# Edge MLP of a graph network: attribute product over 128 rows, bias added on the way out of PSUM, sums three groups behind, padding rows spread

## The reference

```
for i in range(4):
    ef  = silu(concat(h[row], h[col], edge_attr) @ edge_w1[i] + edge_b1[i])
    ef  = silu(ef @ edge_w2[i] + edge_b2[i]) * edge_mask
    agg = segment_sum(ef, row, n)
    h   = (h + silu(concat(h, agg) @ node_w1[i] + node_b1[i]) @ node_w2[i] + node_b2[i]) * node_mask
```

## Time and profile before

| | |
|---|---|
| median of three runs | 8339.4 us (8332.0 to 8347.34) |
| span of the profiled execution | 8339.0 us |
| TensorE matmul busy | 6397.8 us (77%) |
| VectorE busy | 4889.1 us (59%) |
| ScalarE busy | 2862.7 us (34%) |
| GpSimd busy | 5197.0 us (62%) |
| first `eat` product (L1650) of L1 to the last | 2294.4 to 5827.6 us |

### The profile page before, as it was taken

The page is one execution under the profiler, slowest core; times in us unless marked ns, Lnnn a source line. Parts: engine busy times, 40 slices in busy tenths (PEclk is TensorE's granted clock), DMA queues, the critical chain, the costliest instruction groups (busy, mean ns, idle before and its releaser), DMA issues. The chain is left out here.

```text
span 8339.0 us, 233485 instructions
## 1 busy us (share of the span) xinstructions
PE 6397.8 (77%) x55084; PEld 5290.0 (63%) x55143; DVE 4889.1 (59%) x13551; ACT 2862.7 (34%) x8539; POOL 5197.0 (62%) x7407
## 2 busy tenths in 40 slices
PE   2222215767699998999899989999976666888998
PEld 1111113555477776888688868887475556887998
DVE  6333346867556654666466646665432225998998
ACT  3222202545333333333333333333233332222554
POOL 3777755756477776777577757776577774222554
PEclk7555556555599999999999999999555556999999
DMA  5000013434388886888688868887300001332232
GB/s 163 3 3 3 3 38 113 120 96 121 94 223 216 216 204 179 222 222 222 164 222 222 222 163 226 222 222 184 100 6 7 7 7 35 82 82 56 72 73 59
DMA packets 1322718, 1020.15 MB, mean 122 GB/s; under 512 B 479756, under 2 KB 1223586, under 8 KB 1321696
## 3 DMA queue, kind: packets, MB, share of 16 engines
q1 hardware_dynamic: 938010, 667.14, 29.1%
q0 software_dynamic: 134272, 178.98, 11.0%
q10 hardware_dynamic: 250308, 172.51, 7.1%
HBM read 951.88 MB, written 73.77 MB: 123 GB/s over the span
## 5 line engine op out<-in xcount | busy, mean ns | idle before, releaser
L1607 POOL DMA_INDIRECT qg<-q_tab,qidx x2520 | 2388.6, 948 | 928.8 <-issue 692.8
L1762 DVE COPY ps<-b 128x384 f32<-128x384 f32 x1120 | 628.1, 561 | 1355.7 <-ACT h L1727 1348.1
L1156 PE MATMUL ps<-rhs_i,ohi 128*128 128x128 f32 (+2 forms) x8640 | 1215.5, 266 | 210.3 <-issue 198.3
L1156 PEld LDWEIGHTS ps<-rhs_i,ohi 128*128 128x128 f32 (+1 forms) x8640 | 999.1, 162 | 343.2 <-issue 281.9
L1122 POOL COPY near<-x 128x48 bf16 x2160 | 676.0, 351 | 775.9 <-PE ps L1145 433.2
L1676 PE MATMUL ps<-ohm,h 128*128 128x128 f32 x6720 | 1032.1, 290 | 61.3 <-DVE ps L1762 30.7
L1307 POOL DMA_INDIRECT got_m<-y_tab,idx_m x832 | 832.9, 1001 | 344.6 <-issue 246.3
L1720 ACT ACTIVATE h<-ps,b 128x384 f32<-128x384 f32 x1120 | 651.2, 581 | 1049.3 <-PE ps L1658 964.1
L1676 PEld LDWEIGHTS ps<-ohm,h 128*128 128x128 f32 x6720 | 838.5, 191 | 252.0 <-issue 237.0
L406 POOL DMA_INDIRECT list_by_src<-ring,rpos x808 | 783.0, 969 | 333.0 <-issue 254.2
L1781 DVE TENSOR_SCALAR ohm<-iota_row,loc_p,w_p 128x128 f32<-128x128 f32 x3360 | 963.1, 354 | 0.1
(11 more groups left out here) (441 smaller groups left out, 8601.8 us busy)
## 6 DMA issues: line engine op xcount, KB each, us to landing
pb<-p_tab ACTq DMA_DIRECT2D x1680, 96.0 KB
pb<-p_tab SPq DMA_DIRECT2D x1680, 96.0 KB
places<-place_by_turn SPq DMA_DIRECT2D x560, 192.0 KB
places_i<-place_by_meeting SPq DMA_DIRECT2D x360, 256.0 KB, 3.4
places_i<-place_by_meeting SPq DMA_DIRECT2D x720, 128.0 KB, 3.1
qb<-q_tab SPq DMA_DIRECT2D x840, 64.0 KB
qg<-q_tab,qidx POOLq DMA_INDIRECT x2520
nears<-near_by_turn SPq DMA_DIRECT2D x560, 64.0 KB
```

Of the source, the lines that this page charges most:

```text
L1156: m = pe.matmul(ps[:, bass.ds(to[j], width)], ohi[:, h, j, :], rhs[:, h, j, 0:width], start=False, stop=True, skip_group_check=True)
L1607: pool.indirect_dma_start(qg[:, h, j, :], None, q_tab, IndirectOffsetOnAxis(ap=qidx[:, h, j:j + 1], axis=0)).then_inc(m_got[h], 16)
```

## The change

Four things. The `eat` and `we36` tiles become 128 rows high, with rows 36 to 127 zeroed once before the layers, and the product L1650 reads all 128 rows. The bias b2 is no longer seeded into PSUM: VectorE's `add(n)` reads z2, adds b2 and writes h2 in SBUF, and then writes zeros to z2 behind a wait for its own add; ScalarE's silu goes from h2 to h2. `sums` runs three groups behind instead of two, `build_m` two behind instead of one. The padding records get the local node p (their partition), and where the column is beyond the table it becomes p instead of 3199.

```
--- before.py
+++ after.py
-                        dve.memset(padt[:, :, 1:2], FAR).then_inc(s_pad, 1)
+                        v_chain(dve, dve.memset(padt[:, :, 1:2], FAR))
+                        dve.tensor_scalar(padt[:, :, 0:1], padt[:, :, 0:1], iota_p[:, 0:1], None, ALU.add).then_inc(s_pad, 1)
...
                         dve.tensor_copy(loc_p[:, at], banks[4][:, 0:HN])
-                        dve.tensor_scalar(col_p[:, at], banks[5][:, 0:HN], float(NP - 1), None, ALU.min)
+                        then(dve.tensor_copy(col_f[:, 0, :], banks[5][:, 0:HN]))
+                        then(dve.scalar_tensor_tensor(col_f[:, 1, :], col_f[:, 0, :], float(NP), col_f[:, 0, :], ALU.is_lt, ALU.mult))
+                        then(dve.tensor_scalar(col_f[:, 0, :], col_f[:, 0, :], float(NP), iota_p[:, 0:1], ALU.is_ge, ALU.mult))
+                        dve.tensor_tensor(col_p[:, at], col_f[:, 0, :], col_f[:, 1, :], ALU.add)
...
-                eat = sb(f"eat{layer}", [36, U3, GW], BF16, st)
...
                         def second(k, h):
                             n = k * U3 + h
-                            pe.wait_ge(m_seed, s0 + 2 + n)
+                            if layer or here(k, h, 1):
+                                pe.wait_ge(m_zero, g0 + n)
                             pe.wait_ge(m_h1, g0 + n + 1)
...
-                        def sums(k, h):
+                        def sums(k, h, after=2):
                             n = k * U3 + h
                             pe.wait_ge(m_ohm, g0 + n + 1)
-                            pe.wait_ge(m_seed, s0 + 3 + n)
+                            pe.wait_ge(m_zero, g0 + n + after)
+                            pe.wait_ge(m_h2, g0 + n + 1)
...
                             first(k, h)
-                            if here(k, h, 2):
-                                sums(*moved(k, h, -2))
+                            if here(k, h, 3):
+                                sums(*moved(k, h, -3))
                             if here(k, h, 1):
                                 second(*moved(k, h, -1))
...
                         def two(k, h):
                             n = k * U3 + h
-                            if here(k, h, 2):
-                                act.wait_ge(m_sum, g0 + n - 1)
-                            act.wait_ge(m_z2, g0 + n + 1)
-                            act.activation(h2[:, h % 2, :, :], z2.rearrange("p (j f) -> p j f", j=M3), ACT.Silu).then_inc(m_h2, 1)
+                            act.wait_ge(m_add, g0 + n + 1)
+                            act.activation(h2[:, h % 2, :, :], h2[:, h % 2, :, :], ACT.Silu).then_inc(m_h2, 1)
...
-                        def seed(k, h):
+                        def add(k, h):
                             n = k * U3 + h
-                            dve.wait_ge(m_h2, g0 + n + 1)
-                            dve.tensor_copy(z2.rearrange("p (j f) -> p j f", j=M3), b2[:, None, :].to_broadcast([P, M3, HID])).then_inc(m_seed, 1)
+                            if here(k, h, 2):
+                                dve.wait_ge(m_sum, g0 + n - 1)
+                            dve.wait_ge(m_z2, g0 + n + 1)
+                            dve.tensor_tensor(h2[:, h % 2, :, :], z2.rearrange("p (j f) -> p j f", j=M3),
+                                              b2[:, None, :].to_broadcast([P, M3, HID]), ALU.add).then_inc(m_add, 1)
+                            dve.wait_ge(m_add, g0 + n + 1)
+                            dve.memset(z2, 0.0).then_inc(m_zero, 1)
...
                             if here(k, h, 2):
-                                seed(*moved(k, h, -2))
+                                add(*moved(k, h, -2))
                             build(*moved(k, h, 1))
                             indices(*moved(k, h, 5))
-                            if here(k, h, 1):
-                                build_m(*moved(k, h, -1))
+                            if here(k, h, 2):
+                                build_m(*moved(k, h, -2))
...
-            we36 = sb("we36", [36, L * HID], BF16, st)
+            we36 = sb("we36", [P, L * HID], BF16, st)
+            eat = sb("eat", [P, U3, GW], BF16, st)
...
                     v_chain(dve, dve.memset(maskT[:, N:NP], 0.0))
+                    v_chain(dve, dve.memset(eat[:, :, :], 0.0))
+                    v_chain(dve, dve.memset(we36[:, :], 0.0))
```

More of the change, by code:

```diff
@@ L1553, in _ @@
                         root_step(act, b_to + 2)
-        m_idx, m_oht, m_ohm, m_z1, m_h1, m_z2, m_h2, m_sum, m_seed = (
-            sem("m_" + n) for n in ("idx", "oht", "ohm", "z1", "h1", "z2", "h2", "sum", "seed"))
+        m_idx, m_oht, m_ohm, m_z1, m_h1, m_z2, m_add, m_zero, m_h2, m_sum = (
+            sem("m_" + n) for n in ("idx", "oht", "ohm", "z1", "h1", "z2", "add", "zero", "h2", "sum"))
         m_got = [sem(f"m_got{h}") for h in range(U3)]
@@ L1562, in edge_mlp @@
         def edge_mlp(layer, we36, w2, b1, b2):
-            g0, k0, s0 = layer * G3, layer * K3, layer * (G3 + 2)
+            g0, k0 = layer * G3, layer * K3
             def here(k, h, lag=0):
@@ L1636, in _ @@
                         for i in range(7):
-                            m = pe.matmul(banks[i], nothing[:, 0:P], nothing[:, :], start=True, stop=True)
-                        m.then_inc(m_seed, 1)
+                            pe.matmul(banks[i], nothing[:, 0:P], nothing[:, :], start=True, stop=True)
                         to = []
@@ L1693, in _ @@
                         take(K3 - 1, U3 - 2)
+                        sums(K3 - 1, U3 - 3)
+                        second(K3 - 1, U3 - 1)
                         sums(K3 - 1, U3 - 2)
-                        second(K3 - 1, U3 - 1)
-                        sums(K3 - 1, U3 - 1)
+                        take(K3 - 1, U3 - 1)
+                        sums(K3 - 1, U3 - 1, 1)
                     @block.scalar
@@ L1795, in _ @@
                         build(0, 0)
-                        dve.wait_ge(m_seed, s0 + 1)
-                        dve.tensor_copy(z2.rearrange("p (j f) -> p j f", j=M3), b2[:, None, :].to_broadcast([P, M3, HID])).then_inc(m_seed, 1)
                         turns(dve, step, K3, U3)
-                        seed(K3 - 1, U3 - 2)
+                        add(K3 - 1, U3 - 2)
+                        build_m(K3 - 1, U3 - 2)
+                        add(K3 - 1, U3 - 1)
                         build_m(K3 - 1, U3 - 1)
-                        seed(K3 - 1, U3 - 1)
         with ExitStack() as st:
@@ L1977, in _ @@
                             p_chain(pool, pool.tensor_copy(we_part[:, :], we[:, :]))
-                            p_chain(pool, pool.tensor_tensor(we36[:, :], we_part[:, :], mine_of(0), ALU.mult))
+                            p_chain(pool, pool.tensor_tensor(we36[0:36, :], we_part[:, :], mine_of(0), ALU.mult))
                             for q in (1, 2):
@@ L1982, in _ @@
                                 p_chain(pool, pool.tensor_tensor(we_mine[:, :], we_part[:, :], mine_of(q), ALU.mult))
-                                p_chain(pool, pool.tensor_tensor(we36[:, :], we36[:, :], we_mine[:, :], ALU.add))
+                                p_chain(pool, pool.tensor_tensor(we36[0:36, :], we36[0:36, :], we_mine[:, :], ALU.add))
                         if not last:
```

15 lines of the change are left out of this document (9 added, 6 removed).

## The result

The changed kernel takes 8271.4 us, the median of four runs (8268.6 to 8275.9); the kernel before took 8338.1 beside it (8332.0 to 8347.3). The ratio is 0.9921, with a 95% interval of 0.9907 to 0.9934. The forecast was 8257 in a range of 8149 to 8330. The span of the profiled run is 8272.0 us, against 8339.0: 67 us less, where the sum promised 82.

A forecast was written before the change was run, and what follows sets the result against it. The prediction took the latency of z2's bank (second, silu, seed, sums, second), not TensorE's work, as the bound. 8339 - 27 (first layer) - 12 (other layers) - 45 (layer ends) + 2 (once only) = 8257 us, range 8149 to 8330.

The forecast's parts named there:

- A: Likeliest case, whole kernel: the latency ring sets the pace and all summed terms hold; 8257 us, chance 0.60.
- the ends: Last 40 us of each inner layer: empty gathers naming different rows cost what others do, 45 us off.
- the ring: Latency chain of z2's bank, second to sums: round falls to 2.92 us, 27 us off first layer, 12 off others.
- 128 rows: Attribute product on TensorE: its own need falls from 2.71 to 2.52 us; nothing counted beyond the covered loop end.
- D: Rival, edge MLP: TensorE was the bound and the 36-row product's edges count in full; 8149 us, chance 0.05.
- B: Rival, zeros to sums: the hop is 0.13 us in all slots, round 2.84; 8170 us, chance 0.12.
- C: Slower rival: zeros into PSUM cost 0.56 us, or something as long follows the add; 8413 us, chance 0.14.
- I trust the successor, not the row: Zeros into z2, sized from a 400-element SBUF memset's successor: 0.45 us for 384 with hop, 0.415 bare.
- 2.935 in six slots and 2.825 in two, 2.91 on average: Round over the loop's eight slots: zeros to sums takes 0.24 us in six, 0.13 in two.
- Three behind: sums three groups behind: silu leaves the latency chain, and VectorE's next signal is covered by 0.4 us.
- E: Rival, layer ends: slow for another reason than equal rows, so the 45 us stay; 8302 us, chance 0.09.
- Once only: Before the layers: zeroing eat and we36 costs VectorE about 2 us, the new col_p operations nothing; plus 2.

The follow-up runs named there:

- copy: Changed kernel with the zeros written to z2 by a copy from SBUF, not a memset: 10259.9 us on the slower chip, ratio 0.9951 to the kernel before.
- zeros twice: Changed kernel with the zeros written to z2 twice, the second write waiting for the first: 8855.7 us.
- place of the wait: Changed kernel with the wait for the zeros written ahead of the wait for ohm in sums: 8221.1 us, ratio 0.9861 to the kernel before.

## Why the prediction was right, and where its terms were off

The case named likeliest, A, came true in its total, and the sum was 15 us too low. Its largest term, the ends, was right. Its second, 39 us for the ring, was not: the ring gave about 1 in the steady rounds, and the 128 rows, which had no term, some 14. That these partly made up for each other was luck.

- **What bounds.** Right. The new round adds up by the same steps as the old one, and every experiment that lengthened or shortened one hop of the ring moved the round by that hop: +0.063 (copy), +0.533 (zeros twice), -0.066 (place of the wait). D is out: in ring-limited rounds 36 and 128 rows read alike. B did not come from the change itself: the hop of 0.13 in slots 1 to 7 is what the exchange of two waits gives. C is out, although its condition was met, see below.
- **The ring, term by term.** `second` to add 0.038, not 0.09 (the lower bound, 0.04, was right). Add 0.557, as forecast. Hop and zeros 0.533, not 0.45: without a hop of 0.035 that is 0.50, and not 0.415. Zeros to `sums` 0.192, not 0.24. `sums` and `second` 1.607, as forecast. Sum 2.927 against 2.935. The errors of the two hops, 0.05 each, cancelled that of the zeros, 0.08. That was luck. Rival C was to decide from zeros of 0.49 on, and they are at 0.50. With the two hops as forecast the average round would have been 2.92 + 0.08 = 3.00, just over the 2.995 from which C decides.
- **Why the zeros were mis-sized.** The step was "I trust the successor, not the row", read from a memset of 400 elements into SBUF in the earlier trace rows: 0.47 to its successor's start. Here the row is no better a guide: it is 0.378 long, and with a hop of 0.035 the work it stands for would begin 0.12 earlier.
- **The steady part: -16 and not -39.** This is the step that failed: "2.935 in six slots and 2.825 in two, 2.91 on average". Two slots are built as the prediction read them, slots 0 and 2. But in slot 0 TensorE comes late from the end of the loop round: `sums` starts there 0.37 behind the zeros, so a short hop gives nothing. Slots 7 and 0 take 3.42 + 2.51 = 5.93, 0.08 more than two rounds of 2.926, where the sum had 2.935 + 2.825 + 0.08 = 5.84. Slot 2 takes 2.859 and not 2.825; slot 3 has a hop of 0.23 and takes 2.96, for a reason that is not known. The four other slots came out nearly as forecast, 2.926 against 2.935. The eight average 2.931 in the last three layers, where the sum had 2.92; before, they averaged 2.930, where the sum had 2.935 from the windows. That leaves nothing there.
- **The first layer.** The eight slots average 2.953 there, not 2.92, and 3.017 before, which leaves 0.064 x 264 = 17 us, where the sum had 27. The hop from `second` to the add is 0.107 in two of its slots and 0.038 in all others, by which slots 6 and 7 get 0.07 and 0.09 longer than in the other layers. In these two VectorE's wait for m_z2 stands in an instruction of its own ahead of the add, elsewhere on the add itself. One of them in the timeline, 3024.80 - 3024.69:

```profile
3023.86 0.83 PE L1673 MATMUL ps<-w,h 128*128 128x128 f32 x6
...
3024.80 0.56 DVE L1771 TENSOR_TENSOR h<-ps,b 128x384 f32<-128x384 f32 x1 [0.77 <-PE ps L1673]
```

  The first layer had more to give because there the seed's wait stood in an instruction of its own ahead of the weight load; the exchange of two waits in the old kernel got 24 us by that alone.
- **What of the 16 us is the ring's.** The changed kernel with 36 rows tells: its steady rounds take 780.8, 775.3, 775.4 and 774.9 us, together 3106.4. That is 1 us less than before (3107.7), some 12 less in the first layer and 3 to 4 more in each of the others. From there to the changed kernel (3091.9) it is 15 us, by the 128 rows.
- **128 rows.** TensorE's own need fell to 2.51, as forecast (2.52), and was hidden by the ring in seven slots of eight, as forecast. It was not worth nothing: the pair at the loop's end gets 0.10 us. That is 13 us in the old kernel and, by the steady rounds, 15 in the new one (22 by the medians). The prediction counted "nothing beyond the covered loop end" and gave that no term. By the Trainium skill, "TensorEngine Tiling (Array Packing)", Key Properties, a change of mode drains TensorE. The trace agrees in that both gaps, 0.10 each, are gone with 128 rows, and away from the loop's end they are not on the path; that a product over 36 rows counts as such a change is not shown by a run of its own.
- **Three behind.** The silu left the ring, as forecast. Not seen: one more `sums` at each layer's end, 1.2 us a layer.
- **Padding.** -50 and not -45; the cause is shown by taking it in (52 us off the old kernel) and out (59 us on the new one). E is out. The end of a layer now runs at the full pace of the ring, 2.98 a group over the last ten intervals.
- **Once only.** +2, as forecast.
- **Not settled:** the 6 us behind the last product of L1 and what is left of the +7 between the layers. Behind the product, kernels with spread places show 2505.4 to 2511.6 us, those without it 2511.4 to 2512.5. It was not isolated.

## What to carry to other kernels

When a ring of waits sets the pace, price every hop of it and not only its operations; and where an instruction waits for several signals, see to it that the one that comes last is on the work itself or on the last instruction ahead of it, and not in one farther ahead. Here that one exchange of two lines was worth 50 us, three times what the whole change gave in the steady part.

Count for each slot of a loop which waits it has in the built program: slots that are written alike need not be built alike, and one of them may not be on the ring at all. Here a slot that TensorE's own queue holds up was counted as a short round. Then run the parts of a change one by one. Of three ideas in this one, the dullest (which row an empty place reads) gave 52 of 67 us, and the most laborious, the new ring, some 5 (8341 - 52 - 13 = 8276 without it, 8271 with it) until its wait was moved.

## What the runs showed of the hardware that was not expected

- A VectorE memset into PSUM is drawn with a row of 0.378 us that begins 0.155 behind its release. Its price is 0.533, as two in a row show. A copy of the same 384 elements starts after 0.035 and takes 0.561.
- A wait in an instruction of its own, and not on the last one ahead of TensorE's weight load, costs 0.066 us in the changed kernel (0.192 against 0.126) and 0.11 in the old kernel's first layer (0.24 against 0.13 in the earlier trace rows). For VectorE's add it costs 0.07 (0.107 against 0.038). On TensorE the profile puts such a wait down to "issue". The Trainium skill, "Perfetto Trace Analysis", Identifying Dependency Chains, says that instructions which wait on several engines may get such an instruction ahead; it gives no price.
- Gathers in which 128 descriptors name one row of the table take 0.67 us a packet, those of different rows 0.11 to 0.15. On the slower chip it is 0.57 against 0.12, and the ends of the layers take no longer for it.
- Two chips of one kind differ by 24% on the same kernel, 10.3 ms against 8.3. Most of it is in the stage of L1, where one moves 150 GB/s and the other 220, though a packet takes as long on both; the cause stays open.
